# A graph network layer stack on one core: 49 edge chunks, no GpSimd drain at block ends, source rows' products one stage earlier, two weight matrices multiplied in preparation, new orders

## The reference

```python
h = relu(ln(x)); x = x + gcn(h)      # agg = segment_sum(w * h[dst], src) + h / deg
h = relu(ln(x)); x = x + sage(h)     # twice: h = relu(mean(h[src] by dst) @ W_l.T + b + h @ W_r.T)
h = relu(ln(x)); x = x + mlp(h)      # msgs = relu([h[src], h[dst], ea] @ mW1 + mb1) @ mW2 + mb2
                                     # agg = mean(msgs by dst)
                                     # upd = relu([h, agg] @ uW1 + ub1) @ uW2 + ub2 + h, then ln * gamma + beta
h = relu(ln(x)); x = x + neigh(h)    # relu(h @ W_self.T + b + mean(h[dst] by src) @ W_neighbor.T + b)
return x
```

## Time and profile before

| | us |
|---|---|
| median of 3 runs | 5219.02 (5215.02 to 5253.27) |
| span of the profiled execution | 5223.6 |
| busy: PE, DVE, ACT, POOL | 3895.7, 4158.1, 3626.8, 3880.5 |
| setup / gcn / sage1 / sage2 / mlp / mean / final | 336 / 973 / 731 / 669 / 1012 / 709 / 794 |
| mean granted TensorE clock | 0.884 of full |

### The profile page before, as it was taken

How to read it: one execution, slowest core, us unless ns; L and a number is a source line. 1 busy time by engine, 2 the same in 40 slices (tenths; PEclk the granted TensorE clock), 3 DMA queues, 4 the chain that set the end, 5 groups by cost and what they waited for, 6 DMA issues and landing times. The chain is left out here.

```text
span 5223.6 us, 87376 instructions
## 1 busy us (share of the span) xinstructions
PE 3895.7 (75%) x22802; PEld 3063.3 (59%) x22802; DVE 4158.1 (80%) x20654; ACT 3626.8 (69%) x9152; POOL 3880.5 (74%) x3228
## 2 busy tenths in 40 slices
PE   5517877778676668999868978989788886666654
PEld 4415666666455556877756766766566665554443
DVE  7628999999999997777758878888799997766564
ACT  0027989888666766777758877878678886766564
POOL 6777787885677766888866777776588775777777
PEclk9868999999777788999989989999899998878777
DMA  9966777776666665666658889988466663333332
GB/s 229 321 192 191 197 211 203 195 201 159 161 152 154 147 139 143 164 152 158 143 136 260 237 224 245 247 236 210 126 147 144 144 139 74 102 98 98 96 96 62
DMA packets 891584, 878.75 MB, mean 168 GB/s; under 512 B 131160, under 2 KB 671714, under 8 KB 891016
## 3 DMA queue, kind: packets, MB, share of 16 engines
q1 hardware_dynamic: 546568, 575.48, 34.2%
q0 software_dynamic: 224000, 235.91, 26.1%
q10 hardware_dynamic: 120514, 61.79, 4.6%
HBM read 345.71 MB, written 533.16 MB: 168 GB/s over the span
## 5 line engine op out<-in xcount | busy, mean ns | idle before, releaser
L1206 POOL DMA_INDIRECT node<-sage_comb,leadd x400 | 644.7, 1612 | 203.5 <-DMA node<-sage_comb,leadd 104.0
L460 PE MATMUL dense_p<-ident,dense_h 128*128 128x128 f32 x1956 | 336.0, 300 | 373.4 <-ACT dense_h L454 367.1
L454 ACT ACTIVATE dense_h<-dense_x,dense_n_shift,dense_n_rstd 128x128 f32<-128x128 f32 x1304 | 534.8, 487 | 89.1 <-DVE dense_n_shift L443 85.7
L460 PEld LDWEIGHTS dense_p<-ident,dense_h 128*128 128x128 f32 x1956 | 239.8, 151 | 475.7 <-ACT dense_h L454 454.0
L1206 POOL DMA_INDIRECT sums<-mlp_same,leadh x200 | 325.2, 1626 | 139.0 <-issue 80.2
L1206 POOL DMA_INDIRECT node<-gcn_comb,leads x200 | 326.3, 1632 | 105.3 <-issue 49.2
L1206 POOL DMA_INDIRECT sums<-mean_comb,leads x200 | 328.0, 1640 | 95.8 <-DMA sums<-mean_comb,leads 45.7
L470 PEld LDWEIGHTS dense_p<-wT,dense_hT 128*128 128x128 f32 x2608 | 378.8, 209 | 22.8 <-issue 7.4
L470 PE MATMUL dense_p<-wT,dense_hT 128*128 128x128 f32 x2608 | 377.1, 292 | 0.0
L451 ACT ACTIVATE dense_n_std<-dense_n_mean_var,eps 128x4 f32<-128x4 f32 x652 | 188.8, 294 | 216.1 <-DVE dense_n_mean_var L437 213.9
L1041 ACT ACTIVATE dense_hT<-dense_p 128x512 f32<-128x512 f32 x489 | 286.2, 589 | 63.8 <-PE dense_p L460 60.8
(11 more groups left out here) (310 smaller groups left out, 14374.1 us busy)
## 6 DMA issues: line engine op xcount, KB each, us to landing
node<-b SPq DMA_DIRECT2D x400, 256.0 KB
sums<-zero_row SPq DMA_DIRECT2D x400, 256.0 KB
node<-zero_row ACTq DMA_DIRECT2D x50, 1152.0 KB
dense_x<-in_x SPq DMA_DIRECT2D x163, 256.0 KB, 3.3
out<-dense_y SPq DMA_DIRECT2D x163, 256.0 KB
x_src<-xs SPq DMA_DIRECT2D x50, 256.0 KB, 5.7
y_dst<-gcn_y SPq DMA_DIRECT2D x50, 256.0 KB, 3.1
sage_xs<-x_src SPq DMA_DIRECT2D x50, 256.0 KB, 3.9
```

The costliest lines, as they stand in the source:

```text
L454: tiles(lambda t: nc.scalar.activation(out[:, t, :], x[:, t, :], func, bias=b.sh[:, t:t + 1], scale=b.rs[:, t:t + 1])).then_inc(done, 1)
L460: return tiles(lambda t: nc.tensor.transpose(ps[:, t * P:(t + 1) * P], x[:, t, :], ident))
L1206: pool.indirect_dma_start(table, bass.IndirectOffsetOnAxis(ap=leads[:, i * G + c, t:t + 1], axis=0), e.comb[c][:, t, :], None, element_off ...
```

## The change

There are 49 chunks in place of 50: streams 0 to 3 have ten rounds, stream 4 has nine, and padding is 88 edges rather than 600. The tables end right behind the rows used; their last 256 rows are filled by four more DMAs in setup. Every block is closed without a drain of POOL. In sage1 each chunk now also turns h, multiplies it by W1_r and stores the product p instead of h; sage2 loads p, adds the gathered sum on DVE, rectifies, turns, multiplies by W2_r and stores q instead of g; mlp loads q and adds the gathered sum to it. The matrices mW2 and the lower half of uW1 are multiplied in setup, and mb2 with the latter, so that mlp's messages need no `sumT` and `apply` and are combined by rows. All tables `TIMES` are replaced (11 to 45 new numbers a stream; the first two of a stage, the period and `every` of dense streams, are shown). `RD` becomes `RDS[c]` in all end waits, `is_last(i)` becomes `is_last(i, c)`.

```diff
-NCH = -(-E // (G * CH)) * G
+NCH = -(-E // CH)
+RDS = tuple(len(range(c, NCH, G)) for c in range(G))
-ZR = -(-(DUMP + CH) // (P * NCH))
-R = P * NCH * ZR
+ZR = 16
+FILLED = P * NCH * ZR
+R = DUMP + CH
...
-    "gcn": (90000, 75000, (
+    "gcn": (89831, 75029, (
-    "sage1": (66000, 68000, (
+    "sage1": (66152, 67615, (
-    "sage2": (64500, 45000, (
+    "sage2": (81988, 42142, (
-    "mlp": (92000, 85000, (
+    "mlp": (91203, 79811, (
-    "mean": (65000, 66000, (
+    "mean": (66129, 64668, (
-    "final": (77000, 0, (
+    "final": (79247, 79247, (
...
+def fill_tail(eng, table, a, b, row, filled):
+    n = (R - FILLED) // P
+    to = table[FILLED:R, a:b].rearrange("(p z) f -> p z f", z=n)
+    eng.dma_start(to, row.unsqueeze(1).to_broadcast([P, n, b - a])).then_inc(filled, 16)
...
-        block = ctx.enter_context(nc.Block())
+        block = ctx.enter_context(nc.Block(no_gpsimd_drain=True))
...
 # setup_phase
+            pe.wait_ge(weights_ready, 1)
+            nc.tensor.matmul(tps[:, 1, 3 * D:4 * D], mT[:, :], k.wD[:, 4, :], start=True, stop=True)
+            nc.tensor.matmul(tps[0:1, 0, 0:D], mcol[:, :], k.wD[:, 4, :], start=True, stop=True).then_inc(folded, 1)
...
+            dve.wait_ge(folded, 1)
+            nc.vector.tensor_copy(k.wD[:, 2, :], tps[:, 1, 3 * D:4 * D])
...
 # sage1_phase
-        nodes = (ln("x_", after=(("get_xs", 1, 0),), norm_after=(("put_h", 1, 0),))
+        nodes = (ln("x_", after=(("get_xs", 1, 0),))
...
-                    Node("root", SCALAR, 205), Node("self", VECTOR, 1060),
+                    Node("root", SCALAR, 205), Node("self", VECTOR, 1060, after=(("put_x1", 1, 0),)),
...
-                 + [Node("put_h", SYNC, 900, after=(("h_norm", 0, 0),), main=False),
+                 + [Node("put_x1", SYNC, 450, after=(("x1", 0, 0),), main=False),
+                    Node("turn", TENSOR, 560), Node("hT", SCALAR, 500), Node("mix", TENSOR, 1000),
+                    Node("prod", SCALAR, 590, after=(("put_p", 1, 0),)),
+                    Node("put_p", SYNC, 450, after=(("prod", 0, 0),), main=False),
...
 # sage2_phase
-        FILL = ("mix", "combine")
-        nodes = ([Node("turn", TENSOR, 560, after=(("get_h", 1, 0),)),
-                  Node("get_h", SYNC, 450, after=(("turn", 0, 0),), main=False),
-                  Node("hT", SCALAR, 500), Node("mix", TENSOR, 2000, after=(("fetch1", 1, 0),))]
-                 + fetch_nodes(2, "mix")
-                 + [Node("relu", SCALAR, 590, after=(("put_g", 1, 0),)), Node("put_g", SYNC, 450, after=(("relu", 0, 0),), main=False)]
+        FILL = ("plus", "combine")
+        nodes = ([Node("plus", VECTOR, 610, after=(("get_p", 1, 0), ("fetch1", 1, 0))),
+                  Node("get_p", SYNC, 450, after=(("plus", 0, 0),), main=False)]
+                 + fetch_nodes(2, "plus")
+                 + [Node("relu", SCALAR, 590), Node("turn", TENSOR, 560), Node("gT", SCALAR, 500), Node("mix", TENSOR, 1000),
+                    Node("prod", SCALAR, 590, after=(("put_q", 1, 0),)), Node("put_q", SYNC, 450, after=(("prod", 0, 0),), main=False)]
...
+                    nc.vector.tensor_tensor(flat(g[c][:, :, :]), flat(p1[c][:, :, :]), flat(a[c][:, :, :]), ALU.add).then_inc(e.done[c], 1)
...
+                    nc.scalar.activation(flat(g[c][:, :, :]), flat(g[c][:, :, :]), ACT.Relu).then_inc(e.done[c], 1)
...
-                    rows_matmul(nc, e.p[c], hT[c], k.wT[:, 1, :], (k.ident[:, :], lambda t: a[c][:, t, :])).then_inc(e.done[c], 1)
+                    rows_matmul(nc, e.p[c], hT[c], k.wT[:, 3, :]).then_inc(e.done[c], 1)
...
 # mlp_phase
-        nodes = ([Node("turn_g", TENSOR, 560, after=(("get_g", 1, 0),)), Node("gT", SCALAR, 500),
-                  Node("mix_s", TENSOR, 1000), Node("plus_s", VECTOR, 610, after=(("fetch1", 1, 0),)),
+        nodes = ([Node("plus_s", VECTOR, 610, after=(("fetch1", 1, 0), ("get_g", 1, 0))),
...
-                 + edge_tail(True, VECTOR, match_after=(("get_keys", 1, 0), ("add1", 1, 0))) + fill_nodes(FILL)
+                 + edge_tail(False, None, match_after=(("get_keys", 1, 0), ("add1", 1, 0))) + fill_nodes(FILL)
...
-                    nc.vector.tensor_tensor(flat(a2[c][:, :, :]), e.p[c][:, :], flat(a2[c][:, :, :]), ALU.add).then_inc(done, 1)
+                    nc.vector.tensor_tensor(flat(a2[c][:, :, :]), flat(gs[c][:, :, :]), flat(a2[c][:, :, :]), ALU.add).then_inc(done, 1)
...
-                    combine_columns(nc, p, e.same[c], v[c]).then_inc(done, 1)
-                if name == "apply":
-                    pe.wait_ge(done, at.before(i, name))
-                    apply_columns(nc, p, col[c], k.wD[:, 4, :]).then_inc(done, 1)
+                    combine_rows(nc, p, e.same[c], v[c]).then_inc(done, 1)
```

More of the change, by code:

```diff
@@ L703, in _ @@
             pool.wait_ge(index_in, 32)
[L704 to L707, removed]
-                    tiles(lambda t: gather(pool, pace, xs[c][:, t, :], inp["x"], gidx[:, i * G + c, t:t + 1], gathered[c]))
+            for n in range(NCH):
+                i, c = n // G, n % G
+                if i > 0:
+                    pool.wait_ge(kept[c], i * 16)
+                tiles(lambda t: gather(pool, pace, xs[c][:, t, :], inp["x"], gidx[:, i * G + c, t:t + 1], gathered[c]))
         @block.sync
@@ L774, in _ @@
                 fill_rows(act, tb.node, 0, W1, k.zero[:, 0:W1], filled, c)
+            fill_tail(act, tb.node, 0, W1, k.zero[:, 0:W1], filled)
+            for half in (0, D):
+                fill_tail(act, tb.sums, half, half + D, k.zero[:, 0:D], filled)
+            act.wait_ge(rows_in, 32)
+            fill_tail(act, tb.node, W1, WT, k.b12[:, :], filled)
             act.wait_ge(table_step, 2)
@@ L1324, in _ @@
             for c in L:
-                pool.wait_ge(e.added[c], RD * T * 16)
+                pool.wait_ge(e.added[c], RDS[c] * T * 16)
         @block.vector
@@ L1433, in step @@
                     fill_rows(sp, tb.sums, 0, D, k.zero[:, 0:D], e.filled, i * G + c, 4 * q, 4)
-                if name == "get_xs" and not is_last(i):
+                if name == "get_xs" and not is_last(i, c):
                     sp.wait_ge(e.done[c], at.after(i, "self"))
                     load_xs(i + 1, c)
-                if name == "put_h":
-                    sp.wait_ge(e.done[c], at.after(i, "h_norm"))
+                if name == "put_x1":
+                    sp.wait_ge(e.done[c], at.after(i, "x1"))
                     sp.dma_start(chunk_rows(tb.x1s, i, c), flat(x1[c][:, :, :])).then_inc(e.kept[c], 16)
-                    sp.dma_start(chunk_rows(tb.h1s, i, c), flat(h[c][:, :, :])).then_inc(e.kept[c], 16)
+                if name == "put_p":
+                    sp.wait_ge(e.done[c], at.after(i, "prod"))
+                    sp.dma_start(chunk_rows(tb.p1s, i, c), flat(p1[c][:, :, :])).then_inc(kept_p[c], 16)
             for c in L:
@@ L1514, in step @@
                 norm_scalar(nc, act, e.done[c], at, i, "h_", name, e.b[c], k.eps[:, :], h[c], x1[c], ACT.Relu)
-                if name == "sumT":
+                if name == "prod":
+                    wait_rounds(act, kept_p[c], i, 16)
+                    act.wait_ge(e.done[c], at.before(i, name))
+                    nc.scalar.activation(flat(p1[c][:, :, :]), e.p[c][:, :], ACT.Copy).then_inc(e.done[c], 1)
+                if name in ("hT", "sumT"):
                     act.wait_ge(e.done[c], at.before(i, name))
@@ L1529, in step @@
                 c = s
+                if name == "turn":
+                    pe.wait_ge(e.done[c], at.before(i, name))
+                    transpose4(nc, e.p[c], h[c], k.ident[:, :]).then_inc(e.done[c], 1)
+                if name == "mix":
+                    pe.wait_ge(e.done[c], at.before(i, name))
+                    rows_matmul(nc, e.p[c], sumT[c], k.wT[:, 1, :]).then_inc(e.done[c], 1)
                 if name == "spread":
@@ L1602, in step @@
                     return
-                if name == "fetch0" and not is_last(i):
-                    pool.wait_ge(e.done[c], at.after(i, "mix"))
-                if name.startswith("fetch") and not is_last(i):
+                if name == "fetch0" and not is_last(i, c):
+                    pool.wait_ge(e.done[c], at.after(i, "plus"))
+                if name.startswith("fetch") and not is_last(i, c):
                     pair(int(name[5:]), i + 1, c)
@@ L1622, in step @@
                 c = s
+                if name == "plus":
+                    dve.wait_ge(e.side_in[c], (i + 1) * 16)
+                    dve.wait_ge(e.gathered[c], (i + 1) * T * 16)
+                    dve.wait_ge(e.done[c], at.before(i, name))
+                    nc.vector.tensor_tensor(flat(g[c][:, :, :]), flat(p1[c][:, :, :]), flat(a[c][:, :, :]), ALU.add).then_inc(e.done[c], 1)
                 if name == "match":
@@ L1843, in step @@
                     match_keys(nc, dve, k, e, i, c, KD, field(k, i, c, INVD))
-                if name == "sumT":
-                    dve.wait_ge(done, at.before(i, name))
```

(1 more changed line is left out.)

212 lines of the change are left out of this document (109 added, 103 removed), and 361 rows, old and new, of the table TIMES.

## The result

| | before | after |
|---|---|---|
| median of the timed runs | 5218.32 | 5090.23 (5076.97 to 5099.39) |
| span of the profiled execution | 5223.6 | 5075.2 |
| busy: PE, DVE, ACT, POOL | 3895.7, 4158.1, 3626.8, 3880.5 | 3742.7, 4104.3, 3645.4, 3786.5 |
| mean granted TensorE clock | 0.884 | 0.885 |

The ratio is 0.972 (95% interval 0.969 to 0.976). A second measurement of the same two kernels on another chip gave 0.974 (0.971 to 0.978), with medians of 5090.5 and 5227.7 us. The forecast was 5075 us, with a range of 5010 to 5150.

The account below looks back on a forecast made before the run. It took GpSimd's count of indirect DMAs to bound most of the time, with about 350 us of GpSimd idle. Terms -91 - 18 + 8 - 20 - 25 = -146 from 5223.6 gave 5078, 5073 against the median; forecast 5075, range 5010 to 5150.

Parts of the forecast that it names:

- One chunk less, -91: All stages: fewer GpSimd indirect DMAs sum to 95.4 us, less 4 in VectorE-paced sage1; bounds -96 and -80.
- No drain, -18: Stage ends: a drain takes 5 us, in full after sage2, mlp and the last write; 18 us saved, bounds 0 and -30.
- sage1's longer chain, +8: sage1: four more steps before `lead`, about 3.5 us longer per chunk, mostly covered; 8 us lost, bounds 0 and 35.
- mlp's relief, -20: mlp: TensorE falls to about 737 us, so GpSimd waits less; 20 us saved, bounds 0 and -50.
- Dense chunks shifted, -25: sage2 and mlp take some 5 dense chunks from sage1 and mean, 40 us less VectorE there; 25 saved, bounds 0 and -60.
- Setup, -5 of the 91, cover at nothing: Setup: four gathers fewer save 5.0 us; added fills and combined matrix hide under gathers, costing nothing.
- Rival 1: Whole kernel: only the count shrinks and GpSimd's idle time stays, giving 5118 us; chance 0.22.
- Rival 2: sage2 and mlp: VectorE sums of two SBUF operands shut GpSimd out, 67 us back, giving 5142; chance 0.05.
- Rival 3: Block ends: the no-drain flag changes nothing, 18 us lost, giving 5093 us; chance 0.07.
- Rival 4: sage1's chain paid in full (+27), no mlp or dense gain (+45), 30 us of order stalls, giving 5177; chance 0.07.
- Rival 5: mlp and sage1: TensorE's clock stays at 1.2 GHz, stages 180 and 60 us above forecast, giving 5315; chance 0.04.

Follow-up runs that it names:

- Count and drain alone: The kernel before with 49 chunks and no GpSimd drain; products, weights, dense rates and orders unchanged: 5232.6 us, ratio 0.999, where the kernel before takes 5239.2.
- sage1 emptied: The kernel after without sage1's new transpose, its eviction and the product by W1_r, storing h in place of p: 5094.3 us, ratio 0.974 to the kernel before.

## Why the prediction was right, and where it wasn't

The total was 15 us off the median, on the right mechanism only in part: errors of up to 25 us in single stages cancelled, and one term was given a price that it doesn't have by itself.

**One chunk less, -91.** The price of the DMAs holds where nothing but GpSimd decides. final fell by 21.7 us, against 15.3 for the forecast's twelve DMAs and 8.1 for the drain as measured; forecast 772, measured 770.1. gcn fell by 12.6 (954 and 958.3). But the step that added these prices up over all stages as if each stage could simply end sooner is the one that failed. Count and drain alone gave 0 rather than -109: 64 us were gained in four stages and 75 lost in three, 59 of them in mean. GpSimd's work fell as priced, and its idle time, which the forecast left as it was, took it back. The prediction had bounds of -96 and -80 for the count. The weaker should have been about 0, since dense work fills the engines beside the edges: dense work that loses a round's cover has to go somewhere.

**No drain, -18.** 23.6 measured. One drain took 6.0 and 6.2 us between stages, at or just above the upper of the bounds of 3.4 and 6.1; the 5 was low, and the 8.1 at the end of the program was unforeseen. The places were not right. I named sage2 and mlp as full and gcn as 1: it was nothing after sage2, where dense work now runs until 1 us before the stage's end (TensorE had been idle for 27 us there before), 2.8 after mlp, and 6.2 and 6.0 after gcn and mean. The pause after sage2, forecast at 4.4 us, stayed at 10.29. It depends on who is last at each end, and the new orders changed that.

**sage1's longer chain, +8.** Nothing, within the 4 us by which such a stage varies. The stage forecast of 718 failed by 24 for another reason. VectorE, which paces it at 92% to 94%, has 676 us of work before, 678 with count and drain alone (26 dense chunks) and 651 after (22). The 25 us less are the edge chunk at 9 us and two dense chunks at 8; at 93% they are 27 of the 38. What the other 11 are, I can't tell apart from the orders (GpSimd's pauses of over 0.6 us inside the stage fell from 84 to 57 us in all).

**mlp's relief, -20.** TensorE went from 882 to 813 us and not to 740. The five more dense chunks are only part of that: in the lines view the dense products of this stage add up to 329 us against 297, and to some 20 more if the bias products whose records are missing are counted, so 30 to 50 of the 76 us. The rest isn't accounted for. Against count and drain alone, with 36 dense chunks and 892 us of TensorE, the stage is 31 us shorter at four chunks more. This agrees with the direction, but no run has taken the moved products back alone, or tried the new tables without them, so their share isn't shown: that the new tables do most of it by themselves is a rival that stands untested.

**Dense chunks shifted, -25.** This is the mis-sized term. The shift is as forecast (5 expected, 7 found in sage2 and mlp), but I priced it as VectorE's work, 8 us a chunk, floored by GpSimd. Mean lost 36 us: 13 for the chunk by GpSimd's prices, 17.4 because the stretch behind its last scatter shrank from 20.5 to 3.1, drain and all, and the rest in GpSimd's waits. Giving the rates of before back costs 111 us, and the forecast had held anything else in the orders to 20 us either way. What I missed is that the remainder at the end of mean is a chain: 64 us in one experiment, 46 in another. Its row was there to be read in the trace of before, 21.25 us of GpSimd's pause at mean's end with engines half idle, and I had set mean's drain to nothing without asking what the other 15 us were.

**Setup, -5 of the 91, cover at nothing.** 22 us shorter. The cover was gone, as the rows above show: gathers ended at 295.2 and the reciprocals behind the fills at 311.7. Half of the 22 us came with gathers of 1020 rather than 1412 ns, shown in the last section; profiles with the 1412 have a setup of 328 or 329 us. The forecast has no term for it, so some 11 us of the agreement in the total are luck.

**The rivals.** Rival 1, only the count shrinks, at 5118: the kernel that had only this took 5233. Its assumption, that the idle time stays as it is, was the weak one (350 us became 452). Rival 2, two SBUF operands shutting GpSimd out: in sage2, which has the new sum, the lines view has

```profile
L627 POOL DMA_INDIRECT sage_a<-node,gidx x196 | 197.4, 1007 | 67.5 <-DMA sage_a<-node,gidx 45.1 <-DMA node<-sage_comb,leadd 11.9 <-POOLq L932 8.0
```

1007 ns to a gather, and 1001 in sage2 before. Nothing of the 67 us is there. The Trainium skill, SBUF — State Buffer, section Who interferes with whom, has the rule for a GpSimd instruction that reads SBUF; beside the indirect DMAs of this stage the sums show nothing of it. Rival 3, the flag: wrong by 23.6 us. Rival 4, sage1's chain in full: emptied, it gave nothing. Its other half, stalls by the new orders, was on the right subject with the wrong sign: the idle time fell to 299 us. Rival 5, the clock: 0.93 in mlp, from 0.95, and 0.87 in sage1, up from 0.80.

By what was measured, the count and the dense work can't be added up as two terms: the count opens room, and the orders decide whether a stage ends sooner for it.

## What to carry to other kernels

In a kernel with static orders and filler work, the price of the work taken out isn't yet a gain: before adding it up by stage, ask where the filler goes that it covered, and look behind the last main instruction of each stage, above all of the last stage that may carry filler. A remainder there costs the length of its dependency chain, here 64 us where the busiest engine worked for 29. And a change that touches counts and tables at once is to be tested with each alone: here the part that looked like three quarters of the gain gave none without the rest.

## What the runs showed of the hardware

**Gathers beside the one-hot tiles have two prices.** Before, a gather took 1412 ns as long as VectorE built the 16-bit tiles. The tile view of `xs` over the first part of setup in the kernel after, and then in the one with sage1 emptied, whose setup is the same code:

```profile
L627 POOL DMA_INDIRECT xs<-in_x,gidx x91: 1009/1020/1027, 59.7 to 179.0; - x91
```
```profile
L627 POOL DMA_INDIRECT xs<-in_x,gidx x71: 1409/1412/1415, 59.0 to 179.2; - x71
```

1020 ns and 1412, each within 1.1%, over the same 120 us; the kernel after has it twice at 1020, the kernel with only count and drain at 1412. Setup is 317 to 319 us in the four profiles with 1020 ns and the root in its place, and 328 and 329 in the two of 49 chunks with 1412, some 11 us. The chip doesn't decide it, as both occur on each of two chips; whether the execution does or where the program lies, no run shows.

**TensorE's clock fell when work was taken away.** Without sage1's new products TensorE is busy for 476 of 702 us and the granted clock is 0.80; with them, 515 of 697 and 0.87, in the stage rows above. It stands between the two levels of 1.2 and 2.4 GHz in both, and the stage wasn't shorter for having less to do. The Trainium skill, TensorE: Matmul & The Clock Gate, Part 1, has the clock follow the engine's activity; these rows agree.

**Two chips had long stalls.** There the kernel before takes 6112 and 6232 us. In the kernel after with its drain, VectorE stood still in setup six times (the waits view counts 205.6 us; timeline, two of them):

```profile
131.86 0.29 DVE L855 TENSOR_SCALAR hi<-iota,parts 128x252 f16<-128x252 f16 x1 [41.84 <-remote]
177.53 0.29 DVE L855 TENSOR_SCALAR hi<-iota,parts 128x252 f16<-128x252 f16 x1 [42.14 <-remote]
```

No semaphore event ends these waits, some 3.5 us of work lie between these two, and a single gather of `xs` is no slower there (947 ns in the median). In final the same kernel has ten such waits on VectorE, 142 us in all. What the engine waits for, no run here shows.
